# The middle and the last stage of a hybrid attention and experts kernel, rewritten unrolled with another order on every engine

## The chip, the cores and the metric

The kernel runs on one core of a Trainium2 chip. The metric is the device time of one execution in microseconds (us). The kernel before took 1541.78 us, the median of three runs (1541.42 to 1545.99).

## What is computed

The input x has 2 batches of 1024 tokens of 512 channels. Four layers follow, each with a residual and a layer norm (`LN`) ahead of it:

```python
x = x + attn_a(LN(x))     # differential attention with a low-pass filter over time
x = x + ffn(LN(x))        # 8 experts of 16 units, softmax router, the best 2 of 8
x = x + attn_b(LN(x))     # linear attention with one sum over time
x = x + ffn(LN(x))        # the same experts again
```

The change touches what follows `attn_a`: its output projection, both expert layers and `attn_b`. They are, cut to their core:

```python
def attn_b(X):                               # X: LN of the residual stream
    h = layernorm(X) * ln_w + ln_b
    Q, K, V = split(h @ W_in + b_in)         # 3 x 512 columns
    Q, K = rope_half(Q), rope_half(K)        # rotates the first 256 columns of each
    A = sum_over_time((K / norm(K)) * V)     # one row of 512 per batch
    return (A * Q) @ W_out + b_out + X

def ffn(x):
    weights = softmax(x @ router_w.T)        # 8 per token
    gate = weights * (weights is one of the top 2)
    a = silu(x @ down_w)                     # 8 x 16 = 128 units
    return (a * gate per expert) @ up_w
```

## The kernel before

Tokens are cut into NT = 16 tiles of 128 (TB = 8 per batch); a tile lies with its 128 tokens in the partitions and 512 channels along each. The program has four stages one after the other: `normalise`, `attention` (together the first two thirds of the time, untouched here), `middle` and `last`. Names that begin with `m_` or `l_` in a profile row are tiles of `middle` or `last`. Everything is hand-ordered: each engine has its own instruction list, and engines wait for each other through semaphores only (`s_...`), so an instruction that waits holds back all that stands behind it on its engine.

`middle` is a software pipeline over steps s. In step s tile s gets the output projection of `attn_a` (`product(bw, ...)`, 12 matmuls, since each fp32 factor is split into a rounded part and a rest, `aTh` and `aTl`, `woh` and `wol`), the residual (`m_x`), and the statistics of its norm. Tile s-1 goes through the first half of the experts: its normalised form `m_n` is transposed (`pe_turn`, L1298), copied by ACT (`m_n1T`), multiplied with `down` (`pe_down`, L1307) and turned into a gate by ten small DVE operations (`dve_gate`, L1236 to L1248). Tile s-2 goes through the second half: the gated units are transposed (`pe_turn_ga`, L1313), multiplied with `up` (`pe_up`, L1319) and added to the residual (`dve_sum`, L1256); then come the statistics of the two norms ahead of `attn_b`, folded into one, and `h2`. Tile s-3 has `h2` transposed (L1476), split into `hTh` and `hTl`, and projected to K, V and Q, 12 matmuls each (`project`, L1438). Tile s-4 has q transposed (L1505), and K times V summed over time by a matmul with a vector `wr` that holds one over the norm of k (L1512, two passes into bank `ba`).

POOL (GpSimd) does in each step: the two operations of `pool_rstd` on one number per partition (L1268 adds epsilon, L1270 raises to -1/2), six such for the double norm (L1734 to L1741), a load of the rope table of this tile (L1745) and a wait for it, `rotate` of k (L1717 to L1720), two operations for `wr` (L1754, L1755), `res = x2 + n2` and `res + bout` (L1763, L1765; 512 wide), the store of `res` (L1767), and last `rotate` of q. PE's transposes of q (L1505) wait for `s_qr`, which POOL raises at L1773 after that. K and Q share the bank `b0`: Q's projection waits for `s_kb`, DVE's copy of k (L1601).

`last` computes z = qT times `wab` (L1825; `wab` is W_out scaled by the sum over time), adds `res` and runs the experts again. Both stages run their first 8 steps from written-out code, and tiles 8 to 15 from a loop of four steps (`steps`, `Fori`), where a wait compares with a register; `wait_alone` adds an increment of a mark behind such waits.

Of the kernel before, what the change touches and what calls it, by code (L numbers as in the profile page):

```python
# [135 lines left out]
def shape_constants():  # L136
# [27 lines left out]
    which = np.zeros((P, NT, B), f)  # L164
    which[:, np.arange(NT), np.arange(NT) // TB] = 1.0
# [7 lines left out]
def build(nc, a, out):  # L173
# [8 lines left out]
    with ExitStack() as outer:  # L182
# [15 lines left out]
        with ExitStack() as ctx:  # L198
# [979 lines left out]
class Experts:  # L1178

    def __init__(self, nc, ctx, pre, w, mark_pool, mark_dve):
# [21 lines left out]


    def dve_stats(self, dve, t):

# [4 lines left out]

    def dve_norm(self, dve, t):
        dve.wait_ge(self.s_rstd, t.times(1, 1))
        if t.past(2):
# [4 lines left out]
    def dve_top(self, dve, t, hl):
        dve.wait_ge(self.s_h, t.times(1, 1))
        if t.past(2):
            dve.wait_ge(self.s_e, t.times(2, -2))
        self.nc.vector.tensor_reduce(self.top[:, t.c % 2], hl[:, NH:NHL], AX.X, ALU.max, negate=True)\
            .then_inc(self.s_top, 1)

    def dve_gate(self, dve, t, hl):
# [17 lines left out]
        if t.past(2):  # L1246
            dve.wait_ge(self.s_tg, t.times(1, -1))
# [687 lines left out]
```

## Time and profile before

| what | us |
|---|---|
| median of three runs | 1541.78 |
| profiled execution | 1549.16 |
| its span, first to last instruction | 1547.5 |
| PE busy | 1250.2 (81%) |
| DVE busy | 818.9 (53%) |
| ACT busy | 807.8 (52%) |
| POOL busy | 590.7 (38%) |
| mean granted TensorE clock (share of full) | 0.901 |
| busiest of 40 slices of the span, DMA | 140 GB/s |

The profiled execution is one of its own and not among the three runs; its time stands 7.4 us above their median. Busy shares are means over four stages that have different limits, so they say little on one stage; the rows below are cut by stage and by step. `middle` lasts from the first instruction after attention (about 1048 us) to 1421.8 us, `last` from there to 1547.5 us.

### The profile page before, as it was taken

How to read it: one execution, taken by the hardware profiler on the slowest of the kernel's cores; microseconds unless marked ns; L12 is line 12 of the kernel's file. 1: busy time of each engine (PE TensorE's matmuls, PEld its weight loads, DVE VectorE, ACT ScalarE, POOL GpSimd, SP SyncE). 2: the span in 40 equal slices, each digit the busy share in tenths (PEclk: the TensorE clock that was granted, in tenths of full speed). 3: DMA queues.
4: the chain of work that ended last, by engine and by line, in shares of the span. 5: the costliest groups of instructions: out<-in, count | busy, mean ns of one | idle time of the engine just before them, and what ended most of it. 6: DMA issues, size and time to landing. Idle time of an engine off the chain costs nothing. (4 is left out here: it accounts for less than half of the span.)

```text
span 1547.5 us, 21528 instructions
## 1 busy us (share of the span) xinstructions
PE 1250.2 (81%) x6637; PEld 639.5 (41%) x6652; DVE 818.9 (53%) x1438; ACT 807.8 (52%) x1741; POOL 590.7 (38%) x662
## 2 busy tenths in 40 slices
PE   5854799888797897898897888866898887875996
PEld 4622233433333343333433324233676655552543
DVE  5554554743834724725635538236566554542675
ACT  2304587787877876877877897823122111110111
POOL 3434407127145244243253300200477665664121
PEclk9985679999999898998899899887899999897998
DMA  4365520801802604404406203003122211012331
GB/s 137 110 140 89 103 31 21 131 16 42 110 16 66 86 16 90 64 16 96 57 35 93 27 14 111 16 0 114 65 89 68 67 54 64 34 48 82 110 122 41
DMA packets 69358, 104.16 MB, mean 67 GB/s; under 512 B 8448, under 2 KB 34688, under 8 KB 69248
## 3 DMA queue, kind: packets, MB, share of 16 engines
q1 hardware_dynamic: 57472, 69.26, 22.9%
q0 software_dynamic: 7168, 25.17, 4.6%
q10 hardware_dynamic: 4608, 8.39, 1.4%
q8 instruction: 53, 0.87, 0.3%
q14 instruction: 57, 0.47, 0.1%
HBM read 68.85 MB, written 33.95 MB: 66 GB/s over the span
## 5 line engine op out<-in xcount | busy, mean ns | idle before, releaser
L1058 ACT ACTIVATE score<-score,nmax 128x1024 f32<-128x1024 f32 (+7 forms) x512 | 364.8, 713 | 165.6 <-DVE nmax L934 83.2
L1088 ACT ACTIVATE prob<-score 128x1024 f32<-128x1024 f32 (+3 forms) x384 | 297.8, 812 | 39.2 <-PE score L795 24.3
L776 PE MATMUL score<-kst,qst 96*128 96x512 bf16 (+3 forms) x768 | 220.5, 367 | 95.7 <-ACT score L1058 75.3
L937 DVE TENSOR_REDUCE nmax<-score 128x1 f32<-128x640 f32 (+3 forms) x256 | 250.6, 1019 | 81.1 <-PE score L780 77.4
L791 PE MATMUL score<-qst,kst 99*128 99x512 bf16 (+3 forms) x768 | 216.0, 351 | 25.8 <-ACT score L1058 11.0
L934 DVE TENSOR_REDUCE nmax<-score 128x2 f32<-128x256 f32 (+3 forms) x128 | 105.3, 824 | 241.9 <-PE score L780 241.9
L720 PE MATMUL misc<-xnT,wg 128*128 128x512 f32 x256 | 141.1, 651 | 24.3 <-DVE raw L874 16.7
L776 PEld LDWEIGHTS score<-kst,qst 96*128 96x128 bf16 x768 | 63.7, 103 | 222.3 <-ACT score L1058 146.4
L791 PEld LDWEIGHTS score<-qst,kst 99*128 99x128 bf16 x768 | 73.4, 102 | 193.5 <-ACT prob L1088 70.0
L780 PE MATMUL score<-mask_s,identb 128*128 128x128 bf16 x512 | 116.6, 237 | 0.0
L1131 POOL TENSOR_TENSOR sq<-y 128x512 f32<-128x512 f32 x14 | 14.5, 1034 | 253.9 <-DVE y L897 195.1
L795 PE MATMUL score<-mask_t,identb 128*128 128x128 bf16 x512 | 106.8, 233 | 0.0
L1058 ACT ACTIVATION_READ_ACCUMULATOR score<-score,nmax 128x1 f32 x512 | 101.9, 199 | 0.0
L811 PE MATMUL acc<-prob,vg 128*32 128x512 f32 (+3 forms) x768 | 92.2, 555 | 0.0
L1438 PE MATMUL m_b<-m_winh,m_hTh 128*128 128x512 f32 x192 | 86.6, 451 | 2.5 <-DVE m_hTl L1570 2.5
L1109 POOL TENSOR_TENSOR rot<-raw,cos 128x1024 f32<-128x1024 f32 x14 | 32.8, 2342 | 140.5 <-DVE swapped L880 140.5
L811 PE MATMUL acc<-prob,vn 128*32 128x512 f32 (+3 forms) x768 | 82.9, 504 | 0.9
L1438 PE MATMUL m_b<-m_winh,m_hTl 128*128 128x512 f32 x192 | 78.3, 408 | 0.0
L1438 PE MATMUL m_b<-m_winl,m_hTh 128*128 128x512 f32 x192 | 77.7, 405 | 0.0
L720 PEld LDWEIGHTS misc<-xnT,wg 128*128 128x128 f32 x256 | 46.6, 204 | 70.5 <-issue 56.7
L780 PEld LDWEIGHTS score<-mask_s,identb 128*128 128x128 bf16 x512 | 54.3, 106 | 50.5 <-issue 23.9
L1139 POOL TENSOR_TENSOR newton<-rs 128x512 f32<-128x512 f32 x14 | 14.5, 1038 | 144.3 <-ACT rs L1050 144.3
(225 smaller groups left out, 2128.9 us busy)
## 6 DMA issues: line engine op xcount, KB each, us to landing
piece_scratch<-pieces POOLq DMA_DIRECT2D x16, 768.0 KB, 4.1
qst<-piece_scratch SPq DMA_DIRECT2D x48, 256.0 KB, 9.5
kst<-piece_scratch SPq DMA_DIRECT2D x48, 256.0 KB, 19.0
x1in<-in_query SPq DMA_DIRECT2D x16, 256.0 KB, 2.8
v_scratch<-v ACTq DMA_DIRECT2D x16, 256.0 KB, 2.0
vg<-v_scratch SPq DMA_DIRECT2D x8, 512.0 KB, 16.1
att_scratch<-y SPq DMA_DIRECT2D x8, 512.0 KB, 2.7
m_aT<-att_scratch SPq DMA_DIRECT2D x16, 256.0 KB, 3.0
```

Of the source, the lines that this page charges most:

```text
L720: mm = nc.tensor.matmul(misc[:], wg[:, g.slot, c, w], xnT[:, c, bass.ds(base, HALF)], start=(c == 0), stop=(c == KC - 1))
L776: mm = nc.tensor.matmul(score[slot][:, bank, 0:w], qst[0:PIECES, g.slot, pair + k, i * P:(i + 1) * P], kst[0:PIECES, g.slot, pair + k, c0: ...
L780: mm = nc.tensor.matmul(score[slot][:, bank, w - P:w], identb[:], mask_s[:], start=False, stop=True, skip_group_check=True)
L791: mm = nc.tensor.matmul(score[slot][:, k, t0:HALF], kst[0:ROWS, g.slot, pair, j * P:(j + 1) * P], qst[0:ROWS, g.slot, pair, h * HALF + t0: ...
L795: mm = nc.tensor.matmul(score[slot][:, k, t0:t0 + P], identb[:], mask_t[:], start=False, stop=True, skip_group_check=True)
L811: mm = nc.tensor.matmul(acc[head * 32:head * 32 + 32, t0:HALF], v[:, g.slot, j, head * 32:head * 32 + 32], prob[:, pslot, head % 2, t0:HAL ...
L934: nc.vector.tensor_reduce(nmax[:, pair:pair + 2, i:i + 1], src[:, :, 0:(i + 1) * P], AX.X, ALU.max, negate=True).then_inc(s_max, 1)
L937: nc.vector.tensor_reduce(nmax[:, pair, i:i + 1], src[:].rearrange("p a b -> p (a b)")[:, 0:(i + 1) * P], AX.X, ALU.max, negate=True).then ...
L1058: ins = nc.scalar.activation(s, s, ACT.Exp, bias=nmax[:, pair + k, i:i + 1], accum_out=den[:, pair + k, i:i + 1])
L1088: nc.scalar.activation(prob[:, u % NPROB, :, t0:HALF], score[slot][:, :, t0:HALF], ACT.Exp).then_inc(s_exp, 1)
L1109: nc.gpsimd.tensor_tensor(rot[:], raw[:], cos[:], ALU.mult).then_inc(s_cosm, 1)
L1438: mm = mmul(b[:], x[:, c * P:(c + 1) * P], y[:, c, col:col + E], start=(c == 0 and n == 0), stop=(c == KC - 1 and n == 2))
```

## The change

- The loops are gone: `middle` and `last` are written out for all 16 tiles, waits compare with constants, and the marks are gone.
- The rope table of all 8 time tiles (2 MB) is loaded once by SP with the later constants, ahead of `s_constb`, instead of 256 KB per step by POOL; the table `which` is gone.
- Powers: DVE adds epsilon (one operation per tile for the first norm, two for the double norm, L1574 and L1575 of the new file), and POOL raises to -1/2, for the double norm both numbers in one operation (`m_rr`, 128x2).
- `rotate` swaps pairs in one operation of 256 elements that reads with stride -1, instead of two of 128.
- The residual `res` is no longer `x2 + n2` on POOL with `n2` from DVE: DVE makes a scale and a shift (`grow`, `shift`, one number per partition) and ACT writes `res` in one `Identity` activation; POOL adds `bout`.
- Sum over time: DVE multiplies k, one over its norm and v in one operation (into v), POOL adds it to `summed` (512 wide), and PE sums over partitions at the end of each batch with four matmuls of one column (`columns`). The matmul with `wr` of each step is gone. For batch 0 `columns` stands at the end of step 13.
- q's transposes have a bank of their own (`tq`); the gated units are transposed into bank `bu`, which then also takes the product with `up`.
- Another order on every engine in both stages.

```diff
+        v.bn_aggr(self.mv[:, k], self.st[:, k]).then_inc(self.s_stat, 1)
+        dve.wait_ge(self.s_stat, 2 * t + 2)
+        if t >= R:
+            dve.wait_ge(self.s_n1, t - R + 1)
+        v.tensor_scalar(self.rstd[:, k], self.mv[:, k, 1:2], EPS, None, ALU.add).then_inc(self.s_var, 1)
+    def pool_rstd(self, pool, t):
+        pool.wait_ge(self.s_var, t + 1)
+        self.nc.gpsimd.tensor_tensor(self.rstd[:, t % R], self.rstd[:, t % R], self.half[:, 0:1], ALU.pow)\
+            .then_inc(self.s_rstd, 1)
...
+                     (rope[:], a["c_rope"].rearrange("(n p) (two e) -> p n two e", p=P, two=2))]
...
+            def second_norm(t):
+                mean = mv2[:, t % R, 0:1]
+                r = rr[:, t % R]
+                dve.wait_ge(s_r, t + 1)
+                if t >= R:
+                    dve.wait_ge(s_grown, t - R + 1)
+                vec.tensor_scalar(grow[:, t % R], r[:, 0:1], 1.0, None, ALU.add).then_inc(s_grow, 1)
+                vec.scalar_tensor_tensor(shift[:, t % R], mean, -1.0, r[:, 0:1], ALU.mult, ALU.mult)\
+                    .then_inc(s_grow, 1)
+                if t >= 2:
+                    dve.wait_ge(s_t2, t - 1)
+                vec.tensor_scalar(h2[:, t % 2], ex.x2[:, t % R], mean, r[:, 1:2], ALU.subtract, ALU.mult).then_inc(s_h2, 1)
...
+                    var = mv2[:, t % R, 1:2]
+                    vec.tensor_scalar(rr[:, t % R, 0:1], var, EPS, None, ALU.add).then_inc(s_rr, 1)
+                    vec.tensor_scalar(rr[:, t % R, 1:2], var, 1.0 + EPS, EPS * EPS, ALU.mult, ALU.add).then_inc(s_rr, 1)
+                if 0 <= s - 1 < NT:
+                    ex.dve_gate(dve, s - 1, hl)
+                if 0 <= t < NT:
+                    second_norm(t)
+                t = s - 4
+                if 0 <= t < NT:
+                    i = t % 2
+                    dve.wait_ge(s_rinv, t + 1)
+                    dve.wait_ge(s_rk, 3 * t + 3)
+                    dve.wait_ge(s_vb, t + 1)
+                    vec.scalar_tensor_tensor(v[:, i], k[:, i], rinv[:, i], v[:, i], ALU.mult, ALU.mult)\
+                        .then_inc(s_kv, 1)
...
+                t = s - 2
+                if 0 <= t < NT:
+                    act.wait_ge(s_grow, 2 * t + 2)
+                    act.wait_ge(ex.s_x2, t + 1)
+                    if t >= R:
+                        act.wait_ge(s_resd[t % R], t // R * 16)
+                    nc.scalar.activation(res[:, t % R], ex.x2[:, t % R], ACT.Identity, bias=shift[:, t % R],
+                                         scale=grow[:, t % R]).then_inc(s_grown, 1)
...
+            def rotate(t, x, chain):
+                ch = Chain(pool, chain, Step(None, t, 1), 3)
+                left = x[:, t % 2, 0:NROPE]
+                pairs = left.rearrange("p (n two) -> p n two", two=2)[:, :, ::-1]
                 swp = sw[:].rearrange("p (n two) -> p n two", two=2)
...
+                ch.link(g.tensor_tensor(swp, pairs, rope[:, t % TB, 1].rearrange("p (n two) -> p n two", two=2),
+                                        ALU.mult))
+                ch.link(g.tensor_tensor(left, left, rope[:, t % TB, 0], ALU.mult))
                 ch.link(g.tensor_tensor(left, left, sw[:], ALU.add))
...
+            for s in range(NT + 5):
+                t = s - 4
+                if 0 <= t < NT:
+                    pool.wait_ge(s_qb, t + 1)
+                    rotate(t, q, s_rq)
+                if s < NT:
+                    ex.pool_rstd(pool, s)
+                t = s - 2
+                if 0 <= t < NT:
+                    pool.wait_ge(s_rr, 2 * t + 2)
+                    g.tensor_tensor(rr[:, t % R], rr[:, t % R], ex.half[:], ALU.pow).then_inc(s_r, 1)
+                t = s - 4
+                if 0 <= t < NT:
+                    pool.wait_ge(s_kv, t + 1)
+                    if t % TB == 0:
+                        g.tensor_copy(summed[:, t // TB], v[:, t % 2]).then_inc(s_summed, 1)
+                    else:
+                        pool.wait_ge(s_summed, t)
+                        g.tensor_tensor(summed[:, t // TB], summed[:, t // TB], v[:, t % 2], ALU.add)\
+                            .then_inc(s_summed, 1)
+                t = s - 2
+                if 0 <= t < NT:
+                    pool.wait_ge(s_grown, t + 1)
+                    g.tensor_tensor(res[:, t % R], res[:, t % R], bout[:], ALU.add).then_inc(s_res, 1)
+                    pool.wait_ge(s_res, t + 1)
+                    pool.dma_start(res_scr[t], res[:, t % R]).then_inc(s_resd[t % R], 16)
+                t = s - 3
+                if 0 <= t < NT:
+                    pool.wait_ge(s_ss, t + 1)
+                    if t >= 2:
+                        pool.wait_ge(s_kv, t - 1)
+                    g.tensor_tensor(rinv[:, t % 2], ss[:, t % 2], ex.half[:, 0:1], ALU.pow).then_inc(s_rinv, 1)
+                    rotate(t, k, s_rk)
...
+                if 0 <= s - 2 < NT:
+                    ex.pe_turn_ga(pe, s - 2, bu)
+                if 0 <= s - 1 < NT:
+                    ex.pe_turn(pe, s - 1, t0)
+                if 0 <= s - 2 < NT:
+                    ex.pe_up(pe, s - 2, bu)
+                if 0 <= s - 1 < NT:
+                    ex.pe_down(pe, s - 1, hl)
...
+            for s in range(NT + 3):
+                if 0 <= s - 2 < NT:
+                    ex.dve_top(dve, s - 2, hl)
+                    ex.dve_gate(dve, s - 2, hl)
+                if s < NT:
+                    dve.wait_ge(s_z, s + 1)
+                    if s >= R:
+                        dve.wait_ge(ex.s_x2, s - R + 1)
+                    nc.vector.tensor_tensor(ex.x[:, s % R], z[s % 2][:], res[:, s % R], ALU.add).then_inc(ex.s_x, 1)
+                    ex.dve_stats(dve, s)
+                    ex.dve_norm(dve, s)
+                t = s - 2
+                if 0 <= t < NT:
+                    if t >= R:
+                        dve.wait_ge(s_out[t % R], t // R * 16)
                     ex.dve_sum(dve, t, bu)
```

The orders around the places that matter most, each engine's instructions as they stand in its list (the names of new lines are those of the new file).

DVE in a full step of `middle`, before: the copies of k and v stand ahead of the gate.

```order
L1590 BN_STATS m_st<-m_x 128x6
L1592 BN_AGGR m_mv<-m_st 128x2
L1601 TENSOR_TENSOR m_k<-m_b,m_bin 128x512
L1603 TENSOR_TENSOR m_v<-m_b,m_bin 128x512
L1236 TENSOR_TENSOR m_eq<-m_we 128x64
L1237 TENSOR_TENSOR m_gt<-m_we 128x64
```

DVE in the same place now, the end of the gate, the second norm and then k:

```order
L1255 TENSOR_TENSOR m_ga<-m_e,m_gate 128x128
L1509 TENSOR_SCALAR m_grow<-m_rr 128x1
L1510 SCALAR_TENSOR_TENSOR m_shift<-m_mv,m_rr 128x1
L1514 TENSOR_SCALAR m_h<-m_x,m_mv,m_rr 128x512
L1586 SCALAR_TENSOR_TENSOR m_v<-m_k,m_rinv,m_v 128x512
L1596 TENSOR_TENSOR m_k<-m_b,m_bin 128x512
L1600 TENSOR_TENSOR m_v<-m_b,m_bin 128x512
L1543 TENSOR_TENSOR m_q<-m_b,m_bin 128x512
L1549 TENSOR_TENSOR m_hTl<-m_t,m_hTh 128x512
```

The copy of k, for which Q's projection waits, moved from ahead of the gate to behind the gate, the second norm and the product with v.

POOL in `middle` before, from the double norm of one tile to the rotation of k (`m_r` and `m_v` here are `r1`, `r12` and `v2`):

```order
L1734 TENSOR_SCALAR m_r<-m_mv 128x1
L1735 TENSOR_TENSOR m_r<-m_r,m_half 128x1
L1737 TENSOR_SCALAR m_v<-m_mv,m_r 128x1
L1738 TENSOR_SCALAR m_v<-m_v 128x1
L1739 TENSOR_TENSOR m_v<-m_v,m_half 128x1
L1741 TENSOR_TENSOR m_r<-m_r,m_v 128x1
L1745 DMA m_rope<-in_c_rope 128x512
L1717 TENSOR_TENSOR m_sw<-m_k,m_rope 128x128
L1718 TENSOR_TENSOR m_sw<-m_k,m_rope 128x128
L1719 TENSOR_TENSOR m_k<-m_k,m_rope 128x256
L1720 TENSOR_TENSOR m_k<-m_k,m_sw 128x256
```

POOL now, one whole step, from the first norm's power to the rotation of q that opens the next step:

```order
L1215 TENSOR_TENSOR m_rstd<-m_rstd,m_half 128x1
L1696 TENSOR_TENSOR m_rr<-m_rr,m_half 128x2
L1704 TENSOR_TENSOR m_summed<-m_summed,m_v 128x512
L1709 TENSOR_TENSOR xnT<-xnT,bout 128x512
L1711 DMA res_scratch<-xnT 128x512
L1717 TENSOR_TENSOR m_rinv<-m_ss,m_half 128x1
L1679 TENSOR_TENSOR m_sw<-m_k,m_rope 128x256
L1681 TENSOR_TENSOR m_k<-m_k,m_rope 128x256
L1682 TENSOR_TENSOR m_k<-m_k,m_sw 128x256
L1679 TENSOR_TENSOR m_sw<-m_q,m_rope 128x256
L1681 TENSOR_TENSOR m_q<-m_q,m_rope 128x256
L1682 TENSOR_TENSOR m_q<-m_q,m_sw 128x256
```

Eleven operations and a DMA per step stand here now, where 20 operations and two DMAs stood.

PE in a step of `last`, before:

```order
L1825 MATMUL l_z<-xnT,l_qT 128x512 x4
L1298 MATMUL l_t<-ident,l_n 128x128 x4
L1313 MATMUL l_t<-ident,l_ga 128x128
L1307 MATMUL l_hl<-down,l_n1T 128x136 x4
L1319 MATMUL l_bu<-up,l_gaT 128x512
```

PE in a step of `last` now:

```order
L1758 MATMUL l_z<-xnT,l_qT 128x512 x4
L1308 MATMUL l_bu<-ident,l_ga 128x128
L1291 MATMUL l_t<-ident,l_n 128x128 x4
L1312 MATMUL l_bu<-up,l_gaT 128x512
L1300 MATMUL l_hl<-down,l_n1T 128x136 x4
```

The transpose of the gated units goes ahead, and `up` now stands between the transposes of `l_n` and the product with `down`. On DVE, the small maximum `l_top` and the gate of tile s-2 now stand at the start of step s, ahead of the residual `l_x` of tile s, and the power of the first norm is waited for right behind the statistics.

## Rows read from the trace of the kernel before

**Rows 1.** Windows: us, length, busy PE, PEld, DVE, ACT, POOL, clock, DMA share, GB/s.

```profile
1070.30:1114.70 44.40, 32.53 (x119) 25.40 (x119) 22.49 (x63) 6.43 (x20) 12.05 (x24) 0.76 0.23 74
1114.70:1356.10 241.40, 204.54 (x877) 145.95 (x878) 137.97 (x314) 43.16 (x120) 156.44 (x263) 0.94 0.18 61
1356.10:1421.80 65.70, 43.75 (x167) 28.07 (x165) 23.88 (x48) 7.71 (x19) 40.10 (x65) 0.85 0.13 43
```

**Rows 2.** Waits, 980 to 1430: waiting engine, line, releaser: us, times, longest.

```profile
PE m_t L1505 <- POOLq L1773: 43.2, 14, 4.8
```

**Rows 3.** Groups of POOL in `middle`: busy us, mean ns, idle before.

```profile
L1763 POOL TENSOR_TENSOR xnT<-m_x,m_n 128x512 f32<-128x512 f32 x16 | 20.8, 1302 | 4.4 <-POOL m_wr L1755 3.2 <-DVE m_n L1616 0.7
...
L1754 POOL TENSOR_TENSOR m_rinv<-m_ss,m_half 128x1 f32<-128x1 f32 x16 | 13.5, 847 | 2.8 <-POOL m_k L1720 2.2
L1719 POOL TENSOR_TENSOR m_k<-m_k,m_rope 128x256 f32<-128x256 f32 x16 | 12.2, 764 | 2.1 <-POOL m_sw L1718 1.4
...
L1270 POOL TENSOR_TENSOR m_rstd<-m_rstd,m_half 128x1 f32<-128x1 f32 x16 | 9.2, 575 | 2.1 <-POOL m_rstd L1268 1.5
L1718 POOL TENSOR_TENSOR m_sw<-m_k,m_rope 128x128 f32<-128x128 f32 x16 | 8.9, 555 | 2.1 <-POOL m_sw L1717 1.4
```

**Rows 4.** Timeline of PE, a step without a stall: start us, us, instruction.

```profile
1131.12 0.60 PE L1298 MATMUL m_t<-ident,m_n 128*128 128x128 f32 x4
...
1133.78 0.47 PE L1438 MATMUL m_bw<-m_woh,m_aTh 128*128 128x512 f32 x1
...
1136.63 1.02 PE L1319 MATMUL m_bu<-up,m_gaT 128*128 128x512 f32 x2
...
1143.10 0.60 PE L1505 MATMUL m_t<-ident,m_q 128*128 128x128 f32 x4
1143.63 1.02 PE L1512 MATMUL m_ba<-m_k,m_wr 128*2 128x512 f32 x2
...
1147.48 0.60 PE L1298 MATMUL m_t<-ident,m_n 128*128 128x128 f32 x4
```

**Rows 5.** Timeline of PE, two stalls [idle, releaser] and a step's end.

```profile
1240.19 0.66 PE L1505 MATMUL m_t<-ident,m_q 128*128 128x128 f32 x4 [1.92 <-POOLq L1773]
...
1261.22 1.12 PE L1505 MATMUL m_t<-ident,m_q 128*128 128x128 f32 x4 [4.46 <-POOLq L1773]
...
1267.84 0.60 PE L1298 MATMUL m_t<-ident,m_n 128*128 128x128 f32 x4
```

**Rows 6.** Timeline of DVE in `middle`: residual to next sum; a gate operation.

```profile
1104.65 0.69 DVE L1584 TENSOR_TENSOR m_x<-m_bw,m_xin 128x512 f32<-128x512 f32 x1 [1.87 <-PE m_bw L1438]
...
1106.20 0.66 DVE L1256 TENSOR_TENSOR m_x<-m_bu,m_x 128x512 f32<-128x512 f32 x1
...
1260.46 0.73 DVE L1248 TENSOR_TENSOR m_ga<-m_e,m_gate 128x128 f32<-128x128 f32 x1
```

**Rows 7.** Chain of waits, one period of `last`: start us, us, what.

```profile
1490.82 3.43 PE l_z L1825 x8
1494.25 0.45 PE l_t L1298 x4
...
1494.73 0.59 ACT l_n1T L1277
...
1495.36 1.19 PE l_hl L1307 x8
1496.56 0.86 PE l_bu L1319 x2
```

**Rows 8.** Timeline in `last`, one tile's maximum, its exponentials, its gate.

```profile
1490.09 0.17 DVE L1225 TENSOR_REDUCE l_top<-l_hl 128x1 f32<-128x8 f32 x1 [0.54 <-PE l_hl L1307]
...
1490.61 0.20 ACT L1285 ACTIVATION_READ_ACCUMULATOR l_we<-l_hl,l_top 128x1 f32 x1
...
1491.99 0.22 DVE L1236 TENSOR_TENSOR l_eq<-l_we 128x64 f32<-128x64 f32 x1
...
1493.89 0.29 DVE L1248 TENSOR_TENSOR l_ga<-l_e,l_gate 128x128 f32<-128x128 f32 x1
```

More of the change, by code:

```diff
@@ L1440, in product, with project, columns @@
                 return mm
-            pe.wait_ge(s_prep, 1)
+            def project(t, b, part, done):
+                product(b, hTh[:, t % 2], hTl[:, t % 2], winh, winl, part * E).then_inc(done, 1)
+            def columns(b):
+                pe.wait_ge(s_summed, (b + 1) * TB)
+                pe.wait_ge(s_hTl, min(COLS_AT - 2, NT) if b == 0 else NT)
+                if b == 0:
+                    pe.wait_ge(ex.s_half, 2)
+                for c in range(KC):
+                    mm = mmul(t1[:, c:c + 1], summed[:, b, c * P:(c + 1) * P], ones[:], start=True, stop=True,
+                              skip_group_check=True)
+                mm.then_inc(s_col, 1)
+            pe.wait_ge(s_fold2, 1)
             for c in range(KC):
-                for n, b in enumerate((b0, b1, ba)):
+                for n, b in enumerate((b0, b1, tq)):
                     mm = mmul(b[:], lnbb[:, c], win[c][:, n * E:(n + 1) * E], start=(c == 0),
@@ L1518, in _ @@
-            steps(pe, NT, R, 2 * R, NT + 4, body)
-            pe.wait_ge(s_tail, 1)
-            for c in range(KC):
-                mm = nc.tensor.transpose(t1[:, c * B:(c + 1) * B], arow[:, c * P:(c + 1) * P], ident[0:B, 0:B])
-            mm.then_inc(s_tail, 1)
+                t = s - 3
+                if 0 <= t < NT:
+                    pe.wait_ge(s_kb, t + 1)
+                    project(t, b0, 0, s_q)
+                if s == COLS_AT:
+                    columns(0)
+            columns(1)
@@ L1638, in _ @@
-            dve.wait_ge(s_wout, 16)
-            for b in range(B):
-                for c in range(KC):
-                    vec.tensor_scalar(wab[:, b, c], wout[:, c], acol[:, c, b:b + 1], None, ALU.mult)\
-                        .then_inc(s_tail, 1)
+                if s == COLS_AT:
+                    columns(0)
+            columns(1)
         @block.scalar
@@ L1651, in round_a @@
             def round_a(t):
[L1653 to L1658 removed]
+                act.wait_ge(s_in[t % 2], t // 2 * 32 + 32)
+                if t >= 2:
+                    act.wait_ge(s_w, t - 1)
+                nc.scalar.copy(aTh[:, t % 2], aT[:, t % 2]).then_inc(s_aTh, 1)
@@ L1814, in _ @@
         @block.tensor
         def _(pe):
-            def body(s):
-                t = s
-                if t.exists(NT):
-                    pe.wait_ge(s_in[t.slot], t.round(32, 32))
-                    if t.past(2):
-                        pe.wait_ge(ex.s_x, t.times(1, -1))
-                    b = t.c // TB if t.reg is None else pe.snap(t.times(1)) // TB
+            for s in range(NT + 2):
+                if s < NT:
+                    pe.wait_ge(s_in[s % R], s // R * 32 + 32)
+                    if s >= 2:
+                        pe.wait_ge(ex.s_x, s - 1)
```

673 lines of the change are left out of this document (244 added, 429 removed).

## The prediction, written before the changed kernel ran

> **What bounds the kernel now.** I read the windows by stage first, then the waits of `middle`, then one step on each engine in the timeline, and for `last` the chain of waits. The change leaves the first 1048 us alone. In the windows the twelve full steps from 1114.7 to 1356.1 take 241.4 us, 20.1 us a step; the fill before them takes 44.4 us and the drain to 1421.8 takes 65.7 us [rows 1]. PE is busy in 204.5 of the 241.4 us, but a step in which PE never stalls takes 1147.48 - 1131.12 = 16.36 us [rows 4]. What lies between is a wait: 43.2 us in 14 stalls of q's transposes until POOL's queue has done with `rotate` of q [rows 2]. A stall costs more than its length. After one of 1.92 us the four transposes took 0.66 us, as at full clock (0.60 in rows 4); after one of 4.46 us they took 1.12, and from there to the step's end went 1267.84 - 1261.22 = 6.62 us where the undisturbed step needs 1147.48 - 1143.10 = 4.38 [rows 4, 5]: 2.2 us lost to TensorE at its lower level of 1.2 GHz. So `middle` is bound by POOL, whose step is the longest.
>
> `last` is bound by PE and one copy of ACT: 3.43 + 0.45 + 0.59 + 1.19 + 0.86, with 0.08 of issue 6.60 us a tile [rows 7]. In it DVE has the gate's time to spare.
>
> **POOL in `middle`, part by part.** Of its step go the six operations for the double norm but one power, the epsilon of the first norm, the rope load with its wait, one operation of each swap, `wr`, and `x2 + n2`. One 512-wide addition for the sum over time comes. What stays, with the means in the groups [rows 3]: two rotations of three operations of 0.76, the swap included at that price, so 4.6; `rinv` 0.85; two powers of 0.58, so 1.2; two 512-wide operations of 1.30, so 2.6; the store's issue, which I put at the 0.6 of a small operation on this engine (L1270 is 0.575). With 0.1 for each of 12 waits that is 11.0 us. The swap of 256 elements with stride -1 is not in the trace: below it stands 0.555 (128 elements, stride 2), above it twice that, 1.11; I take 0.76, the row of the same 256 elements without a stride. At 1.11 the step costs 0.7 more. POOL's 11 us are far under 20.1, so the old bound is gone by any of these. Unrolled waits alone would give only part of it.
>
> **PE in `middle`.** The matmul with `wr` goes (1.02 us of row length, 0.95 to the next), and the wait for ACT's copy of the transposed norm goes, since `down` now stands behind the 12 matmuls of `product` (about 0.55). PE's floor is 16.36 - 0.95 - 0.55 = 14.9 us a step [rows 4].
>
> **DVE in `middle`: the new bound.** The copy of k moved behind the gate, and Q's projection waits for it. I follow one step from PE's first transpose at 0. The three transposes take about 1.1 us, `product` 1136.63 - 1133.78 = 2.85 [rows 4], so `m_x` starts at 4.2. From `m_x` to past the aggregate is 1.55 (1106.20 - 1104.65, rows 6). Adding epsilon is not in the trace; it lies between 0.1 and 0.22 (the smallest spacing and the whole of a gate operation of rows 8), and I take 0.25 with the wait ahead. The power on POOL is 0.575 plus two handovers of 0.09, 0.75 in all, and nothing of DVE lies beside it but the small maximum: norm at 6.75. The norm passes in 0.45, sum and second statistics in 1.6 (as the 1.55), two small operations 0.25: gate at 9.05. The gate takes 1493.89 + 0.29 - 1491.99 = 2.2 where POOL is quiet [rows 8]; I add 0.4 for one operation held by the power of `m_rr`, since L1248 shows 0.73 in `middle` and 0.29 in `last` [rows 6, 8]. Then `grow` and `shift` 0.25, `h2` 0.45, the product with v 0.6, k 0.7: done at 13.65. Q is ready for PE at 12.0, so PE stalls about 1.7 us; that is under the 1.92 after which the clock stayed. Q's 12 matmuls take 2.9, so the next step begins at 16.6. I take 16.8 for handovers that I can't see. ACT's new 512-wide activation stands beside idle time: ACT is busy in 43.2 of 241.4 us [rows 1]. Only POOL's `res + bout` waits for it, so I cost it at nothing; if that cover went, its 0.6 us would come on top in POOL's step.
>
> The page "SBUF — State Buffer" of the Trainium skill, section "Who interferes with whom", says that a DVE instruction with two SBUF inputs is held by a GpSimd instruction that reads SBUF, and the other way round. L1248 with its two SBUF inputs, 0.73 against 0.29 us, agrees [rows 6, 8]. By that rule the gate is freer now, since POOL's long additions wait for the product with v; without my 0.4 the step is 16.4.
>
> **Ends of `middle`.** In the fill POOL waited for DVE and one step followed the other; now the residual of the next tile no longer waits for the transposed norm, but the gate still lies in the way: I take 42 for 44.4. The rope table is 2 MB at once ahead of the wait of POOL. The busiest of the profile page's 40 slices moved 140 GB/s, so it could take 15 us; POOL's first work waited until DVE had folded the weights, which covers a good part. I take 0, with 10 as the other end. Steps 4 to 15: 12 x 16.8 = 201.6, and 1.5 for `columns` with its five DVE operations at step 13, against 241.4: -38.3. In the drain no `product` and no `m_x` stand ahead of k, so steps 16 to 18 are near PE's own sums: 12.5, 11.2 and 11.5, then q's copy, rotation (2.3), transposes, and the scaling of `wab`, 7.8. That is 43.0 against 65.7: -22.7. `middle` in all: -2.4 - 38.3 - 22.7 = -63.4.
>
> **`last`.** PE's sum loses ACT's copy: 3.43 + 0.30 + 0.45 + 0.86 + 1.19 = 6.2 us. But DVE now stands still while ACT makes the exponentials and while POOL raises to the power. Its round: from the maximum to the end of the exponentials 1490.81 - 1490.09 = 0.72, handover 0.05, gate 2.2 with wait 0.05 [rows 8], `l_x` and statistics 1.6, epsilon 0.25, power 0.75, norm 0.45, sum 0.6: 6.7 us, longer than PE's 6.2 and than the 6.6 of before. Fifteen rounds of +0.1 make 1.5; the gate of a tile starts a step later, so the fill and the drain get longer by about one exponentials, gate and `up` round, 5.5. `last`: +7.
>
> **The sum.** -63.4 + 7 = -56.4 on the profiled execution's 1549.2: 1492.8. That execution was 7.4 us above the median, so the same difference from 1541.8 gives 1485.4; I say 1486.
>
> **Rivals.**
> 1. *PE bounds the step* (15 us). For it: my DVE chain is added from spacings that each could be 0.1 too long, and the gate may be undisturbed. Against it: it needs 1.8 us less in a chain of 9.4. 12 x -1.7 = -20: 1466.
> 2. *POOL closes a loop.* Behind the product with v (12.9 in the step) stand the sum, `res`, the store, `rinv` and both rotations, and only then the next tile's power, which DVE waits for. Nominally 1.4 + 1.4 + 0.9 + 0.95 + 2.4 + 2.4 = 9.5, so POOL is at the power 5.6 into the next step, needed at 6.0: just in time. With a swap of 1.11 and one more 0.5 us it is late by 0.8: 17.6 a step, 1495.
> 3. *The clock falls.* If the chain is 0.8 us or more longer, the stall before Q passes the bracket between 1.92 (clock kept) and 4.46 (clock lost) in rows 5, and each step pays up to 2.2 more: 19.5 to 20, 12 x 3 = +36: 1522.
> 4. *Slower than before.* The same mechanism at its full price: DVE's two-input operations held as in rows 6 (0.44 each for the gate's six and `h2`, the product and the rests, some +3.5 us), the clock loss of 2.2 in every step, the rope table late by 10. Step 16.8 + 3.5 + 2.2 = 22.5: 12 x 5.7 = +68, and +10: 1564. It decides from a step above 21. POOL's long operations would have to run under the gate for that, and they wait for what comes after it.
>
> **Chances.** Forecast 47% (its own range 1476 to 1494), rival 1 17%, rival 2 20%, rival 3 12%, rival 4 4%. The range for 8 in 10 goes from rival 1 to most of the way to rival 3: 1460 to 1512. A change under 0.3% (4.6 us) can't be told from none. Faster 0.95, same 0.01, slower 0.04.
>
> **What will show it.** Right: the steps of `middle` 16.8 us apart, PE's idle time before L1405 of Q's projection with DVE's `m_k` as releaser, 1 to 2 us each, no stall of q's transposes, clock near full; in `last` a period of 6.7 and ACT waiting less. Rival 1: no idle time before Q. Rival 2: `m_n` idle before it for POOL's `m_rstd` by more than 0.8 us, with POOL busy up to it. Rival 3: a granted clock under 0.9 in the steps and transposes of 1.1 us. Wrong altogether: a POOL step of 16 us or more, a table load on ACT in each tile, or a late `s_constb`.

## The result, and the profile after

The changed kernel took 1477.49 us (median of 4 runs, 1475.97 to 1487.37), the kernel before 1543.88 beside it (4 runs, 1541.42 to 1549.28): a ratio of 0.957, 95% interval 0.953 to 0.962. A second set on another chip gave 1479.87 against 1550.2, 0.955 (0.952 to 0.958). The forecast was 1486 with 1460 to 1512, so the time came out 8.5 us lower, inside the range and at the lower end of the forecast's own 1476 to 1494.

The profiled execution took 1487.37 us, its span is 1485.3. The windows of it, cut at the same places of the program as [rows 1], with `last` as the fourth (columns as there):

```profile
1076.60:1119.00 42.40, 31.99 (x118) 24.93 (x119) 23.21 (x73) 8.26 (x22) 7.82 (x11) 0.77 0.22 74
1119.00:1313.50 194.50, 178.34 (x861) 142.18 (x860) 132.40 (x364) 51.03 (x131) 114.04 (x144) 0.99 0.17 60
1313.50:1357.50 44.00, 35.20 (x163) 27.31 (x161) 20.79 (x49) 9.03 (x21) 30.57 (x38) 0.94 0.11 42
1357.50:1485.30 127.80, 104.12 (x368) 54.94 (x368) 79.17 (x272) 22.01 (x80) 18.22 (x33) 0.90 0.29 99
```

| stretch | before | forecast | after |
|---|---|---|---|
| fill | 44.4 | 42.0 | 42.4 |
| 12 steps with `columns` | 241.4 | 203.1 | 194.5 |
| drain | 65.7 | 43.0 | 44.0 |
| `last` | 125.7 | 132.7 | 127.8 |
| sum | 477.2 | 420.8 | 408.7 |

The four stretches give 68.5 us, against the 56.4 that the prediction added up. The untouched first part took 7.3 us more in this execution than in the one profiled of before (`middle` begins at 1055.85, not 1048.5), and the start of `middle` ahead of the fill 1.1 less. PE is busy in 178 of the 194.5 us of the steady part, with the granted clock at 0.99 where it was 0.94.

The wait of [rows 2] is gone. Waits of `middle` now (engine, line, releaser: us, times, longest):

```profile
POOL m_rstd L1215 <- DVE m_rstd L1211: 52.2, 16, 19.6
...
PE m_b L1405 <- DVE m_k L1596: 16.8, 13, 2.0
...
DVE m_n L1226 <- POOL m_rstd L1215: 9.9, 16, 0.8
```

The second row is the wait that the prediction named: Q's projection for DVE's copy of k. One step on PE (start us, us, instruction, [idle before, releaser]) answers to [rows 4]:

```profile
1182.55 0.60 PE L1439 MATMUL m_t<-ident,m_h 128*128 128x128 f32 x4
...
1193.70 0.60 PE L1473 MATMUL m_tq<-ident,m_q 128*128 128x128 f32 x4
1195.53 0.50 PE L1405 MATMUL m_b<-m_winh,m_hTh 128*128 128x512 f32 x1 [1.23 <-DVE m_k L1596]
...
1198.43 0.60 PE L1439 MATMUL m_t<-ident,m_h 128*128 128x128 f32 x4
```

A step is 1198.43 - 1182.55 = 15.88 us, of which 1.23 is the stall; the transposes take 0.60, as at full clock. The same step on DVE, the chain that ends in k:

```profile
1186.51 0.69 DVE L1557 TENSOR_TENSOR m_x<-m_bw,m_xin 128x512 f32<-128x512 f32 x1 [0.52 <-PE m_bw L1405]
...
1189.06 0.55 DVE L1226 TENSOR_SCALAR m_n<-m_x,m_mv,m_rstd 128x512 f32<-128x512 f32 x1 [0.64 <-POOL m_rstd L1215]
...
1191.32 0.22 DVE L1243 TENSOR_TENSOR m_eq<-m_we 128x64 f32<-128x64 f32 x1
...
1191.77 0.23 DVE L1246 TENSOR_TENSOR m_eq<-m_eq,tri 128x64 f32<-128x64 f32 x1
...
1193.54 0.15 DVE L1509 TENSOR_SCALAR m_grow<-m_rr 128x1 f32<-128x1 f32 x1
...
1194.79 0.68 DVE L1596 TENSOR_TENSOR m_k<-m_b,m_bin 128x512 f32<-128x512 f32 x1
```

And on POOL, which is done with q's rotation 0.28 us before it can start on the next tile's power:

```profile
1183.07 0.73 POOL L1679 TENSOR_TENSOR m_sw<-m_k,m_rope 128x256 f32<-128x256 f32 x1
...
1185.51 1.07 POOL L1679 TENSOR_TENSOR m_sw<-m_q,m_rope 128x256 f32<-128x256 f32 x1
...
1187.46 0.72 POOL L1682 TENSOR_TENSOR m_q<-m_q,m_sw 128x256 f32<-128x256 f32 x1
1188.47 0.55 POOL L1215 TENSOR_TENSOR m_rstd<-m_rstd,m_half 128x1 f32<-128x1 f32 x1 [0.28 <-DVE m_rstd L1211]
1191.48 0.74 POOL L1696 TENSOR_TENSOR m_rr<-m_rr,m_half 128x2 f32<-128x2 f32 x1 [2.46 <-DVE m_rr L1575]
```

One step is not like this: the one after `columns` of batch 0. There DVE first scales `wab` (first row), `m_x` comes 4.76 us behind the first transpose and not 3.96, PE's stall grows to 2.03, and behind it Q's matmuls soon start 0.43 apart, where they start 0.23 apart in the other steps:

```profile
1279.30 2.63 DVE L1523 TENSOR_SCALAR xnT<-xnT,m_acol 128x512 f32<-128x512 f32 x4
```

```profile
1293.18 0.50 PE L1405 MATMUL m_b<-m_winh,m_hTh 128*128 128x512 f32 x1 [2.03 <-DVE m_k L1596]
...
1294.95 0.63 PE L1405 MATMUL m_b<-m_winh,m_hTh 128*128 128x512 f32 x1
1295.38 0.63 PE L1405 MATMUL m_b<-m_winh,m_hTl 128*128 128x512 f32 x1
```

The twelve take 1297.51 - 1293.18 = 4.33 us in place of 2.90, at a granted clock of 0.63 (window 1293.2 to 1297.5).

In `last`, one period on PE, to be read against [rows 7]:

```profile
1410.24 0.33 PE L1308 MATMUL l_bu<-ident,l_ga 128*128 128x128 f32 x1 [0.39 <-DVE l_ga L1255]
1410.40 0.60 PE L1291 MATMUL l_t<-ident,l_n 128*128 128x128 f32 x4
1410.92 1.12 PE L1312 MATMUL l_bu<-up,l_gaT 128*128 128x512 f32 x2
1411.88 1.09 PE L1300 MATMUL l_hl<-down,l_n1T 128*128 128x136 f32 x8
1412.81 3.60 PE L1758 MATMUL l_z<-xnT,l_qT 128*128 128x512 f32 x8
1416.79 0.33 PE L1308 MATMUL l_bu<-ident,l_ga 128*128 128x128 f32 x1 [0.38 <-DVE l_ga L1255]
```

The period is 6.55 us, with PE waiting 0.38 for DVE's gate; DVE itself stands idle twice, 0.59 for the exponentials and 0.69 for POOL's power:

```profile
1412.73 0.55 DVE L1226 TENSOR_SCALAR l_n<-l_x,l_mv,l_rstd 128x512 f32<-128x512 f32 x1 [0.69 <-POOL l_rstd L1215]
...
1414.54 0.23 DVE L1243 TENSOR_TENSOR l_eq<-l_we 128x64 f32<-128x64 f32 x1 [0.59 <-ACT l_we L1277]
```

### The profile page after: what moved, and what is told of

The parts are those of the page before. It is cut to its first block and busy times, and to the rows that moved or that the text cites. A ratio compares the mean times of both kernels' runs of the same rounds, so it can differ in the third digit from the quotient of the medians.

```text
span 1485.3 us, 20587 instructions
## 1 busy us (share of the span) xinstructions
PE 1224.6 (82%) x6617; PEld 636.3 (43%) x6632; DVE 814.1 (55%) x1518; ACT 821.2 (55%) x1757; POOL 529.8 (36%) x487
## 5 line engine op out<-in xcount | busy, mean ns | idle before, releaser
L789 PE MATMUL score<-qst,kst 99*128 99x512 bf16 (+3 forms) x768 | 221.8, 359 | 25.1 <-ACT score L1056 9.7
L793 PE MATMUL score<-mask_t,identb 128*128 128x128 bf16 x512 | 111.3, 240 | 0.0
L1405 PE MATMUL m_b<-m_winh,m_hTh 128*128 128x512 f32 x192 | 84.1, 438 | 18.2 <-DVE m_k L1596 16.8
```

Of the source, the lines that this page charges most:

```text
L789: mm = nc.tensor.matmul(score[slot][:, k, t0:HALF], kst[0:ROWS, g.slot, pair, j * P:(j + 1) * P], qst[0:ROWS, g.slot, pair, h * HALF + t0: ...
L793: mm = nc.tensor.matmul(score[slot][:, k, t0:t0 + P], identb[:], mask_t[:], start=False, stop=True, skip_group_check=True)
L1405: mm = mmul(b[:], x[:, c * P:(c + 1) * P], y[:, c, col:col + E], start=(c == 0 and n == 0), stop=(c == KC - 1 and n == 2))
```

## The experiments

The total carries the untouched first part, which varied by over 10 us between profiled executions (first `m_x` at 1061.8 to 1073.4 in kernels with the same code up to there). So each kernel is also compared by three lengths read from its profile: the mean step (8 steps, from the fifth `m_x` of DVE to the thirteenth), the stretch from the first `m_x` to the sixteenth, and the tail from there to the end of the span. These lengths vary too where nothing was changed: the changed kernel, A2, E4 and E6 have the same `middle`, and their steps agree within 0.01 us, but their stretches lie between 225.5 and 228.2, the difference being in the first three steps. The tail holds the drain of `middle` and the whole of `last`.

| kernel | ratio to before (95%) | step | stretch | tail |
|---|---|---|---|---|
| before | 1 | 19.18 | 273.4 | 207.2 |
| E3 before, unrolled | 0.981 (0.977 to 0.984) | 17.64 | 249.3 | 203.9 |
| E9 E3, rope resident | 0.966 (0.961 to 0.971) | 16.63 | 237.2 | 188.8 |
| changed | 0.957 (0.953 to 0.962) | 15.92 | 228.2 | 183.7 |
| changed again (A2) | 0.955 (0.952 to 0.958) | 15.92 | 228.2 | 185.2 |
| E1 k ahead of the gate | 0.953 (0.949 to 0.956) | 15.65 | 221.4 | 185.4 |
| E2 k and product ahead | 0.948 (0.944 to 0.951) | 15.33 | 217.5 | 185.7 |
| E5 one pad | one run, 1487.78 us | 17.05 | 237.4 | 184.4 |
| E5 three pads | one run, 1531.71 us | 19.93 | 272.2 | 189.3 |
| E7 swap in two | 0.958 (0.954 to 0.961) | 16.81 | 233.4 | 185.3 |
| E4 old order in `last` | 0.957 (0.953 to 0.961) | 15.92 | 226.4 | 180.9 |
| E6 sum under the exponentials | 0.950 (0.947 to 0.954) | 15.91 | 225.5 | 178.6 |
| E8 E2 and E6 | 0.943 (0.940 to 0.946) | 15.33 | 215.7 | 175.9 |

### E3 and E9: which part of the change brings what

The kernel before with its loops written out, and then also with the whole rope table loaded once:

```diff
-            steps(pool, NT, R, 2 * R, NT + 4, body)
+            steps(pool, NT, R, NT, NT + 4, body)      # and so on every engine, in both stages
...
+                      (rope[:], a["c_rope"].rearrange("(n p) (two e) -> p n two e", p=P, two=2))]
...
-                    pool.dma_start(rope[:, i], a["c_rope"]...)
```

> The kernel before with both stages written out for all 16 tiles and nothing else. Theory A (POOL's work per step bound the old middle stage; the loop only added to it): the written-out steps 5 to 8 of before took 17.6 to 19.5 us on POOL against 21.1 in the loop, so steps 4 to 15 come to 12 x 18.3 = 220 us instead of 241, and the whole to about 1521. Rival B (the loop's register waits were the main cost): the steps fall to PE's own 16.4, 197 us, and the whole to about 1495. Last stage unchanged at 126 us in both.

> As e3_before_unrolled, with the rope table resident (2 MB loaded once by SP with the later constants; the one-row tile arow lies in sq to make room), the swap still in two operations and every order as before. Theory A: POOL loses a DMA issue, a gap and a landing, 3.6 us of 18.3, so it is at 14.7 and PE's own 16.4 a step binds: steps 4 to 15 take 197 us, nearly what the full change has (194.5), and the whole is about 1495. Rival B (the new order on the engines made the gain): the steps stay at 18 us or more, over 216 us.

E3 took 1515.82 us, E9 1490.78, against 1547.25 of before on that chip. Both came out as theory A had it: in E3 the steps fall to 17.64 in the mean, not to PE's 16.4, and in E9 to 16.63. In E3 POOL is still the longest, and its step holds a wait for the table (timeline of POOL, and of PE at q's transposes, E3):

```profile
1199.91 0.86 POOL L1745 DMA_DIRECT2D m_rope<-in_c_rope  x1 [0.30 <-POOL m_r L1741]
```

```profile
1195.81 0.66 PE L1505 MATMUL m_t<-ident,m_q 128*128 128x128 f32 x4 [1.39 <-POOLq L1773]
```

The next rotation starts at 1203.24, after 2.47 us of idle time for that DMA. In E9 q's transposes no longer wait, and PE's own sum with the matmul of `wr` and a wait of 0.57 for ACT's copy of the transposed norm is the step, 16.63 us; this one row shows the transposes without a stall:

```profile
1200.86 0.60 PE L1506 MATMUL m_t<-ident,m_q 128*128 128x128 f32 x4
```

So of the 4.3 points of the change, unrolling stands for 1.9 and the rope table, put on top of it, for 1.4. The last 0.9 come from the new order with the shorter PE step and the other powers, residual and sum; E9's interval and the changed kernel's only just touch, and the profiles show 9.0 us in the stretch and 5.1 in the tail. By the two lengths of the profiles together the three parts are 27.4, 27.2 and 14.1 us, so the split between the first two is rough. The table was not tried without the unrolling, and the parts of the rest were not run one by one.

### E1 and E2: taking the wait for k away

E1 puts DVE's copy of k ahead of the gate. E2 puts the product with v there too, has POOL do `rinv` and k's rotation ahead of `res + bout`, and ACT the square of k ahead of the residual:

```diff
...                                                        # E2: the product with v stands here
+                    vec.tensor_tensor(k[:, i], b0[:], bin_[:, E:2 * E], ALU.add).then_inc(s_kb, 1)
                 if 0 <= s - 1 < NT:
                     ex.dve_gate(dve, s - 1, hl)
```

> The changed kernel with DVE's copy of k moved ahead of the gate, all else the same. Theory A, with the loop through POOL: PE's stall of 1.23 us before Q goes, but the product with v comes 0.6 later and the whole of POOL's chain behind it (9.3 us from the end of the product to the end of q's rotation) with it, so DVE waits longer for the power of the norm: the step is 16 to 16.6, no gain or up to 0.6 us a step slower (total 0 to +8). Rival B, DVE's copy of k alone bound it: the step falls to PE's own 14.65 us, total -15.

> The changed kernel with the product with v and the copy of k ahead of the gate on DVE, the square of k ahead of the residual on ACT, and the power and rotation of k ahead of the residual on POOL. Both theories: neither PE's stall nor POOL's chain is left on the path, the step falls from 15.9 to PE's own 14.65, and steps 4 to 15 from 194.5 to about 179: total about -15 against the changed kernel. If DVE-POOL contention rises (rotations of k now run under the gate, whose operations read two tiles in SBUF), the gate grows from 2.2 by up to 2 us; the end of h2 at 12.3 then comes to 14.3, still under 14.65, so no more than 0.3 us a step.

E1: after three steps of 13.9 to 14.7 us the step settles at 16.0, no better than 15.88. POOL is at the power with no idle time ahead, and DVE waits for it (timelines of POOL and DVE, E1):

```profile
1161.08 0.73 POOL L1686 TENSOR_TENSOR m_q<-m_q,m_sw 128x256 f32<-128x256 f32 x1
1161.89 0.55 POOL L1215 TENSOR_TENSOR m_rstd<-m_rstd,m_half 128x1 f32<-128x1 f32 x1
```

```profile
1162.48 0.55 DVE L1226 TENSOR_SCALAR m_n<-m_x,m_mv,m_rstd 128x512 f32<-128x512 f32 x1 [4.03 <-POOL m_rstd L1215]
```

The expectation said that PE's stall before Q would go. It did not: it is 1.37 where it was 1.23, because the copy of k stands behind the norm that waits for POOL (timeline of PE, E1):

```profile
1165.47 0.50 PE L1405 MATMUL m_b<-m_winh,m_hTh 128*128 128x512 f32 x1 [1.37 <-DVE m_k L1584]
```

This is the loop of rival 2: with k out of the gate's way, a loop through POOL that is as long takes over, so moving k alone was worth nothing in the settled step. The stretch is 6.8 us shorter all the same: the steps before POOL's loop closes, and those around `columns`, where the stalls stay under 1 us and the clock is kept. (The 15.65 of the table is a mean of short and settled steps.) The intervals of E1 and the changed kernel overlap. E2 opens the loop: the product no longer stands behind the gate, and POOL has 0.56 us of slack ahead of the power. The step is 15.4 in most steps and 14.6 in a few, not the 14.65 expected, because POOL's sum and rotation now run under the gate (timeline of DVE, then PE, E2):

```profile
1165.39 0.22 DVE L1243 TENSOR_TENSOR m_eq<-m_we 128x64 f32<-128x64 f32 x1
1165.52 1.31 DVE L1244 TENSOR_TENSOR m_gt<-m_we 128x64 f32<-128x64 f32 x1
...
1167.40 0.63 DVE L1248 TENSOR_TENSOR m_gt<-m_gt,m_eq 128x64 f32<-128x64 f32 x1
...
1169.97 0.15 DVE L1509 TENSOR_SCALAR m_grow<-m_rr 128x1 f32<-128x1 f32 x1
```

```profile
1170.70 0.66 PE L1439 MATMUL m_t<-ident,m_h 128*128 128x128 f32 x4 [0.80 <-DVE m_h L1514]
```

The gate took 1169.97 - 1165.39 = 4.6 us in place of the 2.22 of the changed kernel, and PE's 14.65 plus the wait of 0.80 for `h2` is the step.

### E5: how far the stall before Q may grow

```diff
+                    for n in range(1):                      # 3 in the other kernel
+                        vec.bn_stats(padst[:, n], bout[:])
                     vec.tensor_tensor(k[:, i], b0[:], bin_[:, E:2 * E], ALU.add).then_inc(s_kb, 1)
```

> The changed kernel with one more 512-wide statistics instruction on DVE ahead of the copy of k in every step of `middle` (some 0.7 us; its result is unused). (A) DVE's chain to k sets the step: 15.88 + 0.7 = 16.6 us, PE's stall ahead of Q's projection from 1.23 to about 1.9 us, clock kept; `middle` some 9 us longer. (B) POOL's loop sets it already, with k only near it: the step grows by less than 0.4.

> The changed kernel with three such instructions ahead of the copy of k (some 2.1 us). (A) the clock stays, only the wait grows: PE's stall about 3.3 us, step 18.0. (B) the prediction's rival 3: the stall takes the clock with it, transposes take 1.1 us in place of 0.6, and the step is up to 2.2 longer still, 20.2.

With one pad the stall is 1.83 in every step, yet the steps are either 16.5 or 18.0, with one or two of the short between two of the long. Windows of three of them, E5 with one pad:

```profile
1139.66:1156.15 16.49, 14.65 (x71) 11.68 (x72) 11.67 (x32) 4.29 (x12) 9.68 (x13) 1.00 0.19 66
1156.15:1172.60 16.45, 14.62 (x71) 11.68 (x72) 11.67 (x32) 4.30 (x12) 9.69 (x13) 1.00 0.18 64
1172.60:1190.63 18.03, 16.19 (x72) 12.82 (x72) 11.18 (x32) 4.30 (x12) 9.67 (x13) 0.91 0.17 59
```

DVE and POOL are not busy for longer in the third; PE is busy 1.55 us more at a clock of 0.91: behind that stall, Q's matmuls start 0.43 apart where they start 0.23 apart elsewhere. With three pads (stall 3.01) the clock held for the first steps and was then lost in each:

```profile
1130.50:1148.10 17.60, 14.61 (x71) 11.64 (x71) 12.30 (x34) 4.24 (x12) 9.23 (x12) 1.00 0.17 60
1148.10:1167.30 19.20, 16.21 (x71) 12.77 (x71) 12.32 (x34) 4.28 (x11) 9.70 (x13) 0.89 0.17 56
1167.30:1187.60 20.30, 17.30 (x71) 13.68 (x71) 12.32 (x34) 4.29 (x11) 9.85 (x13) 0.84 0.15 52
```

A pad costs DVE 0.6 us, not 0.7 (the stall grew from 1.23 to 1.83 and 3.01), and the step grew by the pad wherever the clock held: 16.47 and 17.6. So DVE's chain to k is the bound, as (A) of the run with one pad had it; its "clock kept" did not hold in every step. In the mean 1.8 us of DVE's time cost 19.93 - 15.92 = 4.0 us a step, (B) of the run with three. What is slow is Q's projection behind the stall, and with three pads the first transposes of the next step (0.96 us for the four of `h2` instead of 0.60). Each of the two kernels ran once, so these readings compare steps within one execution.

### E7: how loose is POOL's loop

```diff
...
-                ch.link(g.tensor_tensor(swp, pairs, rope[:, t % TB, 1].rearrange("p (n two) -> p n two", two=2),
-                                        ALU.mult))
+                ch.link(g.tensor_tensor(swp[:, :, 0], pairs[:, :, 1], sn[:, :, 0], ALU.mult))
+                ch.link(g.tensor_tensor(swp[:, :, 1], pairs[:, :, 0], sn[:, :, 1], ALU.mult))
```

> The changed kernel with each rotation's swap on POOL as two operations of 128 elements in place of one of 256 (the same numbers; about 0.55 + 0.1 more per rotation, 1.2 to 1.3 us of POOL in a step). (A) POOL's loop (product with v, sum, residual, store, inverse, both rotations, then the next tile's power) has only the 0.28 us of slack that the changed kernel shows ahead of the power: DVE's norm waits up to 1 us longer for POOL, and the step goes from 15.88 to 16.8 or so, as rival 2 had it; 13 x 0.9 = 12 us. (B) POOL's loop is loose (the rotations give way): the step stays within 0.2 of 15.9.

The step is 16.81 in the mean, the figure of (A), but not by (A)'s way alone: a POOL that is late in each step and no change of clock would give 15.88 + 0.67 = 16.6. From the second late step on POOL is late in every other step only (timelines of POOL, DVE and PE, E7):

```profile
1160.54 0.55 POOL L1215 TENSOR_TENSOR m_rstd<-m_rstd,m_half 128x1 f32<-128x1 f32 x1
```

```profile
1161.13 0.55 DVE L1226 TENSOR_SCALAR m_n<-m_x,m_mv,m_rstd 128x512 f32<-128x512 f32 x1 [1.31 <-POOL m_rstd L1215]
```

```profile
1167.60 0.50 PE L1405 MATMUL m_b<-m_winh,m_hTh 128*128 128x512 f32 x1 [1.91 <-DVE m_k L1596]
1168.27 0.63 PE L1405 MATMUL m_b<-m_winl,m_hTh 128*128 128x512 f32 x1
```

0.67 us of POOL's lateness lengthens PE's stall to 1.91, the clock falls behind it, and that step is 18.1; the next is 15.9 again, since POOL caught up meanwhile. So that the mean meets the forecast is partly luck. The stretch is 5.2 us longer than that of A2 and the median 3.6, less than the 12 expected: the first three steps and the end of the stretch, where POOL has slack, pay nothing. The intervals of E7 and A2 overlap, so the total alone would not show it; the rows do.

### E4 and E6: `last`

E4 gives the changed kernel the order of before in `last`. E6 moves DVE's sum of tile s-3 to stand between the small maximum and the gate of s-2:

```diff
                 if 0 <= s - 2 < NT:
                     ex.dve_top(dve, s - 2, hl)
+                t = s - 3
+                if 0 <= t < NT:
+                    if t >= R:
+                        dve.wait_ge(s_out[t % R], t // R * 16)
+                    ex.dve_sum(dve, t, bu)
+                if 0 <= s - 2 < NT:
                     ex.dve_gate(dve, s - 2, hl)
...                                                        # the sum of s-2 behind the norm goes
```

> The changed kernel, with the order of before in `last` (exponentials of a tile made in the step ahead of its gate, the gate's transposes in a bank of their own). `middle` is untouched. (A) The prediction's account of `last` (the later gate lengthens the fill and the drain, the period is near that of before): the period goes from 6.55 back to 6.60 us, the stage from 127.8 to about 125.7, so -2 +- 1 us on the changed kernel. (B) the rival, the new order gains by its shorter PE sum (6.2): the old order is slower, by 15 x 0.3 = 4 us or more.

> The changed kernel; in `last` DVE makes the sum of tile s-3 while ACT makes the exponentials of s-2, in place of standing idle 0.59 us for them at each tile. `middle` is untouched. (A) DVE's round bounds `last` with its two waits (0.59 for the exponentials, 0.69 for POOL's power): the period goes from 6.55 to PE's sum of 6.2 or so, the stage gets shorter by 15 x 0.35 = 5 us. (B) PE bounds it: the period stays at 6.5 to 6.6, and the time as well. (C) the sum frees its bank later or in front of PE's up projection: longer, at most by 0.5 us a tile.

The tail holds the drain of `middle` too, so `last` is also read by itself, from the second tile's `l_z` on PE to the end of the span: 109.7 us before, 111.7 and 111.3 in the changed kernel's two profiles, 109.2 in E4, 104.8 in E6. E4 has a period of 6.60, and its `last` is 2.1 to 2.5 us shorter than the changed kernel's, as (A) had it. Its ratio can't be told from theirs. E6's period alternates between 5.96 and 6.29, 6.12 in the mean, its `last` by this measure is 6.5 to 6.9 shorter, and DVE no longer waits for the exponentials: its sum stands in that place (timeline of DVE, E6):

```profile
1405.88 0.16 DVE L1233 TENSOR_REDUCE l_top<-l_hl 128x1 f32<-128x8 f32 x1
1405.96 0.68 DVE L1263 TENSOR_TENSOR l_x<-l_bu,l_x 128x512 f32<-128x512 f32 x1
...
1406.63 0.23 DVE L1243 TENSOR_TENSOR l_eq<-l_we 128x64 f32<-128x64 f32 x1
```

### E8 and A2: the best version

> The changed kernel with the order of e2 in `middle` (product with v and copy of k ahead of the gate) and that of e6 in `last` (the sum under the exponentials). (A) the two gains are apart and add up: steps of 14.6 to 15.4 us, `last` at 6.1 us a tile, 6 us under e2: a ratio of about 0.943 to before. (B) PE, now with hardly a stall, is granted less of its clock, and part of the gain goes: ratio 0.948 or above.

> The changed kernel itself once more, beside e7 and e8 on one chip, for the comparison. By its first runs: 0.957 of the kernel before, steps of 15.88 us, `last` at 6.55 a tile.

E6's ratio and the changed kernel's two have overlapping intervals, so E6's gain rests on these rows and on E8.

E8 took 1462.07 us (6 runs) where A2 took 1479.87 and before 1550.2 on the same chip. The gains add up, as (A) had it: step and stretch are about those of E2, the tail is shorter than E6's. It beats both kernels, with intervals well apart.

## Why the prediction was right, point by point

- **The bound moved from POOL to DVE's copy of k: right.** Pads on that chain lengthen every step by at least their whole time (E5). But it is not alone: in E1, with k moved, POOL's loop holds the step at 16.0. Rival 2's sum (POOL ready 5.6 into the step, needed at 6.0, a slack of 0.4) was nearly exact: POOL is ready at 5.64, needed at 5.92, a slack of 0.28, and it decides as soon as k is moved or POOL slowed (E1, E7). Part of that is luck, since the product with v, POOL's loop and the step were each put too long and the errors cancel.
- **The step, 16.8 forecast, 15.88 measured**, is the term that was mis-sized, by 12 x 0.92 = 11 us. From the first transpose, k was to be done at 13.65 and was at 1195.47 - 1182.55 = 12.92. `m_x` started at 3.96, not 4.2: the prediction's own parts were 1.1 + 2.85 = 3.95, and it wrote 4.2 without a reason. From there to the norm 2.55, forecast and measured; to the gate 2.26 for 2.3. The gate took 2.22, not 2.6: the 0.4 for a gate operation held by POOL's power was not there, as L1246 at 0.23 beside the power of 1191.48 to 1192.22 shows. The rest, 0.07, is in the small operations. The 0.2 added for handovers had no counterpart.
- **The 0.4 came from a misread row.** The prediction took it from L1248 at 0.73 [rows 6] and put it down to a power. In that trace the gate operation of 1260.46 stands beside the last addition of q's rotation (timeline of POOL, before):

```profile
1260.31 0.72 POOL L1720 TENSOR_TENSOR m_q<-m_q,m_sw 128x256 f32<-128x256 f32 x1 [0.18 <-POOL m_q L1719]
```

- **16.4 was nearer.** The prediction gave it beside the port rule of the Trainium skill ("SBUF — State Buffer", "Who interferes with whom"), by which a DVE instruction with two inputs in SBUF contends with a GpSimd instruction that reads SBUF. E2's trace agrees, since POOL's long sum there does hold a gate operation (1.31 us). The power of the changed kernel does not: it reads SBUF as well, and L1246 with its two inputs in SBUF kept its 0.23 beside it.
- **`columns`, 1.5 forecast, about 3.5 measured**: 1.3 on PE itself, 0.8 by which DVE's scaling delays `m_x`, and 1.4 from the clock behind a stall of 2.03. So the 12 steps came out 8.6 us below the forecast and not 11; the two wrong terms partly cancel.
- **POOL's step**: POOL is busy 114.04 / 12 = 9.5 us a step; the forecast's 11.0 without its 1.2 of waits and 0.6 of issue is 9.2. The swap with stride -1 took 0.73 for k, as taken (0.76), not the 1.11 of the other end. For q it took 1.06 (median of 12), which makes up the 0.3. That is not the stride: it starts beside DVE's split of `aT` (L1500, 1.01 us), and in E2, where another operation of q's rotation stands there, the contiguous multiplication took the 1.07. The single swap mattered more than the sum showed: with two operations in its place the loop is late (E7).
- **Unrolled waits alone give part of it: right** (E3). What the prediction did not price apart is the rope wait, 1.0 us of each step in the mean (E3 to E9) and 15 us of the tail.
- **The rope table at nothing: right as far as the fill shows**, 42.4 for 42. ACT's residual (0.81 us) at nothing: the step has no wait in which it is last.
- **The drain** 44.0 for 43.0.
- **`last`**: +7 forecast, +2.1 measured. DVE's round is 6.55, not 6.7, so 15 rounds gained 0.7 instead of losing 1.5; that leaves 2.8 us for the later gate in fill and drain, against 5.5, and E4, which takes it back, agrees in direction and size.
- **The total.** The four stretches came out 12.1 us below the forecast (+0.4, -8.6, +1.0, -4.9), the median 8.5; the rest is within what the untouched first part varies by.
- **Rival 3** was set from a bracket of one stall of 1.92 with the clock kept and one of 4.46 with it lost. E5 and E7 show the clock lost behind stalls of 1.83 and 1.91 too, in some steps and not in others. The forecast's stall of 1.7 lay closer to this edge than the prediction allowed for; the measured 1.23 kept the clock in every step, and the changed kernel lost it once, behind the 2.03 of the step after `columns`. Why it was kept behind one stall and lost behind the next of the same length is open.

## What to carry to other kernels

When the longest engine is relieved, add up the whole loops through the other engines and not only each engine's own sum: here DVE's chain, POOL's loop and PE's floor lay within 1.3 us of each other, and moving k alone gained nothing in the settled step. A step that comes once a batch needs the same sum: `columns` cost more than twice its forecast. An idle slot that is short and comes once a tile (a wait for exponentials of 0.59) is best filled with an operation that is ready, as E6 did for some 6 us. Unrolling and a resident table brought three quarters of the gain, with the order as it was.

## What the runs showed of the hardware

- One stall of some 1.8 us a step can cost nearly as much again. Where it was 1.83 in each step (E5, one pad), 1.55 us of slower matmuls came in every second or third step; behind 1.91 (E7) the same came each time but the first; behind 2.03 (changed kernel) 1.4 us, once; behind 3.01 (E5, three pads), after two steps that kept the clock, some 2.8 in each (20.4 in place of 17.6), though only 1.6 in the first of these. Stalls of 1.23 (changed kernel) and 1.37 (E1) in each step kept it.
- A DVE operation of 64 elements took 1.31 us instead of 0.22 while POOL added 512-wide rows (E2); beside POOL's power on two numbers such an operation kept its 0.23 (changed kernel, L1246).
- POOL read 256 fp32 elements with the two of each pair swapped (stride -1) at the price of contiguous ones, 0.73 us; two operations of 128 with stride 2 took 0.52 each (E7).
